# Reordering VectorE's and ScalarE's steps in the 16x64 attention layers: turned copies first, combining multiply last, copy of the last pair ahead of the exps

## What is computed

```python
h = (x - mu) * rsqrt(var + eps) * ln_scale + ln_bias
q, k, v = up-projections of h @ w_down_q.T and h @ w_down_kv.T, (b, 16, s, 64)
q, k = rope(q), rope(k)
scores = einsum('bhqd,bhkd->bhqk', q, k) / sqrt(64)
attn = softmax(scores, axis=-1)
out = einsum('bhqk,bhkd->bhqd', attn, v)
out = out.reshape(b, s, 1024) @ w_out.T + residual
```

## Time and profile before

| | |
|---|---|
| time, median of 3 runs | 2920.61 us (2910.09 to 2923.78) |
| the profiled execution | 2914.34 us, its span 2912.6 us |
| PE busy | 2224.6 us (76%) |
| DVE busy | 1690.1 us (58%) |
| ACT busy | 1174.3 us (40%) |
| POOL busy | 522.7 us (18%) |

### The profile page before, as it was taken

How to read it: one execution, slowest core, us unless ns; L and a number is a source line. 1 busy time by engine, 2 the same in 40 slices (tenths; PEclk the granted TensorE clock), 3 DMA queues, 4 the chain that set the end, 5 groups by cost and what they waited for, 6 DMA issues and landing times. The chain is left out here.

```text
span 2912.6 us, 40706 instructions
## 1 busy us (share of the span) xinstructions
PE 2224.6 (76%) x13779; PEld 1382.4 (47%) x13779; DVE 1690.1 (58%) x3810; ACT 1174.3 (40%) x2898; POOL 522.7 (18%) x703
## 2 busy tenths in 40 slices
PE   4668888789996897534799994936888886898982
PEld 2424343367774454423566663625555654344441
DVE  5568999633434562877456556562665554754524
ACT  3114444445552564211344441410555553354550
POOL 1122220000002410121111101011333322212100
PEclk9759999899997898866899997965999998698995
DMA  0043323110002310000000001011000001332200
GB/s 27 12 116 86 115 77 92 50 40 1 1 1 62 76 46 28 8 0 0 31 1 1 1 1 28 1 27 34 1 1 1 1 1 38 85 75 63 53 11 17
DMA packets 109272, 95.63 MB, mean 33 GB/s; under 512 B 61414, under 2 KB 96526, under 8 KB 105742
## 3 DMA queue, kind: packets, MB, share of 16 engines
q1 hardware_dynamic: 75790, 91.99, 12.2%
q10 hardware_dynamic: 33280, 1.05, 0.5%
HBM read 77.21 MB, written 14.81 MB: 32 GB/s over the span
## 5 line engine op out<-in xcount | busy, mean ns | idle before, releaser
L920 DVE TENSOR_REDUCE L_xattn_mx<-L_xattn_psS 128x1 f32<-128x512 f32 x512 | 326.9, 684 | 152.9 <-PE L_xattn_psS L1045 148.7
L1160 ACT ACTIVATE L_xattn_PT<-L_xattn_psT 128x512 f32<-128x512 f32 x512 | 284.7, 598 | 170.8 <-PE L_xattn_psT L1057 163.6
L1071 PE MATMUL L_xattn_psO<-L_xattn_PT,L_xattn_V 128*32 128x256 f32 x2048 | 264.1, 404 | 40.8 <-DVE L_xattn_PT L931 40.8
L588 ACT ACTIVATE L_attn_pr<-L_attn_psS,L_attn_negm 128x256 f32<-128x256 f32 (+1 forms) x512 | 222.4, 447 | 175.4 <-PE L_attn_psS L511 92.0
L1045 PE MATMUL L_xattn_psS<-L_xattn_KR,L_xattn_QR 72*128 72x512 bf16 x512 | 224.0, 441 | 56.3 <-DVE L_xattn_mx L920 30.0
L1057 PE MATMUL L_xattn_psT<-L_xattn_QR,L_xattn_KR 75*128 75x256 bf16 x1024 | 198.7, 283 | 3.0 <-ACT L_xattn_PT L1160 2.0
L1875 DVE TENSOR_TENSOR L_ffn_wt<-L_ffn_act,L_ffn_cw 128x512 f32<-128x512 f32 x128 | 88.5, 692 | 183.8 <-ACT L_ffn_act L1992 172.4
L1071 PEld LDWEIGHTS L_xattn_psO<-L_xattn_PT,L_xattn_V 128*32 128x32 f32 x2048 | 118.4, 115 | 154.6 <-issue 61.2
L931 DVE SCALAR_TENSOR_TENSOR L_xattn_PT<-L_xattn_PT,L_xattn_floor_w 128x512 f32<-128x512 f32 x256 | 178.4, 741 | 16.1 <-DMA L_xattn_floor_w<-L_xattn_staged_floor 11.6
L392 DVE TENSOR_REDUCE L_attn_mx<-L_attn_psS 128x2 f32<-128x512 f32 x256 | 164.4, 684 | 40.0 <-PE L_attn_psS L501 40.0
L415 DVE TENSOR_TENSOR L_attn_aoT<-L_attn_raw,L_attn_psOR 128x256 f32<-128x256 f32 x128 | 54.0, 422 | 222.7 <-ACT L_attn_raw L601 222.7
(11 more groups left out here) (537 smaller groups left out, 4342.8 us busy)
## 6 DMA issues: line engine op xcount, KB each, us to landing
L_xattn_KR<-L_xattn_k_parts SPq DMA_DIRECT2D x96, 192.0 KB
L_xattn_floor_w<-L_xattn_staged_floor SPq DMA_DIRECT2D x8, 2048.0 KB, 8.2
L_xattn_QR<-L_xattn_q_parts SPq DMA_DIRECT2D x32, 288.0 KB
L_xattn_k_parts<-L_xattn_ks SPq DMA_DIRECT2D x48, 128.0 KB, 2.6
L_xattn_ctxT<-in_ctx SPq DMA_DIRECT2D x24, 192.0 KB, 2.4
L_attn_QR<-L_attn_q_parts SPq DMA_DIRECT2D x16, 288.0 KB
L_attn_KR<-L_attn_k_parts SPq DMA_DIRECT2D x48, 96.0 KB
L_xattn_q_parts<-L_xattn_qs SPq DMA_DIRECT2D x48, 64.0 KB, 2.5
```

What stands on the lines that cost most here:

```text
L588: ins = nc.scalar.activation(pr[n % 3][:, r, t, 0:width], psS[(2 * n + r) % 3][:, t, 0:width], ACT.Exp, bias=negm[:, n % 4, t, r:r + 1], s ...
L920: nc.vector.reduce_max(mx[:, b % 2, u, hd:hd + 1], psS[n % 2][:], AX.X).then_inc(s_used, 1)
L1071: ins = nc.tensor.matmul(psO[r:r + HW, g % 2], V[b % NV][:, kt, n % H], PT[(n * NU + kt // 2) % NPT][:, kt % 2], start=(kt == 0), stop=(kt ...
L1160: nc.scalar.activation(PT[i % NPT][:], psT[i % NPS][:], ACT.Exp).then_inc(exp_ready, 1)
```

## The change

VectorE's step becomes `copy_turned(n-2)` (causal), `maxima(n)`, the reads, `invert(n-1)`, `combine(n-2)`, and then the moments where the step has them: the multiply comes last in the step, and it is the pair n-2 instead of n-3. ScalarE's step becomes (`copy_turned(n-2)` in the layer that is not causal), the reads, `copy_out(n-2)`, `exps(n)`: the last two change places. No instruction is added or removed, and the orders of TensorE, GpSimd and SyncE stay. The two layers share the function, so both change.

```diff
@@ VectorE @@
             for n in range(FIRST, LAST):
-                if 0 <= n - 3 < NN:
-                    combine(n - 3)
                 if causal and 0 <= n - 2 < NN:
                     copy_turned(n - 2)
                 if 0 <= n < NN:
...
                 if 0 <= n - 1 < NN:
                     invert(n - 1)
+                if 0 <= n - 2 < NN:
+                    combine(n - 2)
                 b, at = n // NP + 2, n % NP
@@ ScalarE @@
                     for job in group:
                         read(job)
+                if 0 <= n - 2 < NN:
+                    copy_out(n - 2)
                 if 0 <= n < NN:
                     exps(n)
-                if 0 <= n - 2 < NN:
-                    copy_out(n - 2)
```

## The result

The changed kernel takes 2933.88 us (median of 7 runs, 2933.12 to 2941.62) against 2916.97 us before (7 runs, 2910.09 to 2923.78), a ratio of 1.0064 with a 95% interval of 1.0048 to 1.0080. Measured once more beside other runs of the kernel before it was 2938.06 against 2915.19, ratio 1.0085 (1.0071 to 1.0099). So it is slower, by 17 to 23 us; 26 were forecast. In absolute time the forecast was 2947 us: 2933.88 lies in its range of 8 in 10 (2929 to 2967) and at the foot of the forecast's own (2934 to 2962). 3.6 us of the distance are the base, 2920.61 us in the three runs that the forecast started from and 2916.97 in seven. The first profile of the changed kernel has a span of 2938.7 us, 26.1 more than before, the second one 2932.0.

What follows compares the result with a forecast made beforehand. The prediction took a circle through ScalarE's copy and VectorE to bound causal plain steps, and TensorE the other layer. Causal -11.8 and other +38 made +26 on 2920.61, so 2947 us, 8-in-10 range 2929 to 2967.

Steps and rivals of the forecast that it cites:

- Both readings: Causal plain steps: a closed circle (exps, copy, multiply, turned copies, maxima, mask, exps), 5.23 us; other layer: TensorE never idles, 4.19.
- The new path, 0.48 + 0.25 + 1.06 or 1.17: `spread_inverse` to copy, copy to exps, exps to next `scores`: 1.79 us in the causal layer, 1.90 in the other.
- The causal layer, -11.8: Sum for the causal layer over plain, T, V or O steps and last pairs: -11.8 us, ends -6 and -15.
- Plain steps: Causal layer, steps without a V job: 4.62 us against 5.23, -0.61 each in 16 steps, -9.8.
- T steps: Causal layer, 7 steps with a T job: two transposes add 0.44 us, so -0.2 each, -1.2.
- (c): Causal layer, 37 steps with V or O, TensorE's own: 1.79 us for 1.73, +0.06 each, +2.2.
- The end of the layer: Causal layer's last pairs, with no projection, circle-bound throughout: between 0 and -4 us, taken as -3.
- The other layer, 61 x 0.65 = 39.7: Non-causal layer, steps n = 2 to 62: `spread_inverse` to next `scores` from 1.25 to 1.90 us, +0.65 each, +39.7.
- the clock: Non-causal layer: some nine steps lose 1.6 us at the lower clock; part of the new wait lies under it, -2.
- the second rival: Non-causal layer: steps fall differently and slow stretches go, 9 x 1.6 = 14.4 us less, 2933; chance 0.06.
- The first rival: Non-causal layer: new 0.65 gap puts six more V and seven T steps at low clock, +21 us, 2968; chance 0.12.
- The rival on the other side: Non-causal layer: earlier multiply brings VectorE's P bank reads forward, returning 48 us of TensorE's waits, 2899; chance 0.07.

Runs made afterwards that it cites:

- the wait alone: Kernel before, with the non-causal layer's exps of pair n also waiting for `spread_inverse(n-2)`, copy still behind them: 2941.31 us, ratio 1.0094.
- the doubled copy: Changed kernel with ScalarE's copy made twice in the non-causal layer, first into a spare tile, both ahead of exps: 2957.00 us against 2938.06.
- The runs with `weigh` moved: Non-causal layer's `weigh` and `spread_inverse` ahead of V, T, C jobs: 2866.03 us on kernel before, 2850.22 with the copy between the heads, 2879.03 on changed kernel.
- the copy between the heads: Kernel before, with ScalarE copying pair n-2 between first and second head's exps of pair n, in both layers: 2898.44 us, ratio 0.9947.

## Why the prediction was right, and where it was off

What bounds a step. Both readings held: one engine's part alone showed the circle over ScalarE's copy in the causal layer, and in the other the wait alone and the doubled copy showed that what is put ahead of the exps is paid in every step.

The new path, 0.48 + 0.25 + 1.06 or 1.17. Measured 0.48, 0.27 and 1.06 (1573.71, 1574.19, 1574.46, 1575.52), and 0.47, 0.27 and 1.17 in the other layer. Right to 0.02.

The causal layer, -11.8. It gave -14.3, with the terms off both ways. Plain steps are 4.73 and not 4.62: `spread_inverse` comes 2.92 after `scores` and not 2.83, since from the P job to `weigh` it is 1.06 where no V job stands between (1571.85 to 1572.91, the P job of the step shown above), and I had put 0.97, the distance from P to V. That is 16 x 0.11 = 1.8 less. T steps are 4.95 for 5.06 forecast, since the two transposes add 0.22 to a plain step and not 0.44: 7 x 0.11 = 0.8 more. V steps are 5.59 for 5.57 forecast, 0.7 less over the 37 steps of (c). The seven steps with V and O went from 7.55 to 7.38, not to 7.61: V had waited for VectorE's read of the O bank (the weight load of V idles 0.39 us for it at n = 27, and not at all after the change), which was late because of the circle, and I had counted that as TensorE's own time; 7 x 0.23 = 1.6 more. The end of the layer gave 5.6 (1.0 in the last step, 4.6 after it) where I took 3, an estimate with little under it.

The other layer, 61 x 0.65 = 39.7. Taking out the excess of the slow V steps over the others of their kind, it is 378.2 before (392.6 less nine of 1.6) and 417.4 in the second profile (420.9 less 0.95, 0.97 and 1.58): +39.2.

The step that failed in size is the clock. I took nine slow V steps to stay nine and put -2 for them. They were seven in one profile and three in the other, with 9.0 and 3.5 us lost in them in place of 14.4. So the term was -5 and -11, and with the causal layer's 2.5 that covers what the forecast of 26 was too high by; it goes part of the way to the second rival, which I gave 0.06. Probably this is more than the chance of two executions: the four profiles in which the plain step of this layer has its old 4.18 and `weigh` its old place show eight or nine slow V steps, the four with the change three, four, four and seven. Why there are fewer stays open, and the kernels with the wait alone and with the doubled copy, at ten and eight, do not have fewer. The first rival, more slow steps for the new gap in every step, did not occur.

The rival on the other side had it that VectorE's reads, and with them 48.3 us of TensorE's waits, would come earlier. They didn't: TensorE waits 30.6 us in 15 for V as before. The change does not move the multiply in VectorE's queue, as this rival has it. In time it does come earlier, released by the earlier copy (it starts at 2237.30 and the next `scores` at 2238.26, n = 31), and the reads come no sooner for it. The runs with `weigh` moved show that most of the 48 us are there to be had: the wait ahead of V falls to 10.2 us in 15, those ahead of T and C go, and the steps get 36 us shorter. It is TensorE's order that holds them, not VectorE's.

What I did not see is that the VectorE part of the diff is no move at all but for the moments. The forecast was not hurt by it, since its sum costs ScalarE's order alone and gives the multiply's move no term.

## What to carry to other kernels

An instruction with a late wait should not stand ahead of the one that releases the bounding engine; put it behind the first such release (here between two heads), where it costs neither engine. The same edit can cut a circle in one variant of a shared function and hang the pace on TensorE's last task in another, so make such orders conditional and read one step of each variant. And before costing a move, count its place in the queue in both versions: a change of step together with a change of index can be no move.

## What the runs showed of the hardware

A gap of 2.07 us in TensorE's work before V brings the clock down to 1.2 GHz in some steps and not in others of the same kind: nine of fifteen in the kernel before, eight with the causal layer changed alone, eight with VectorE's part alone (in six of its V steps the gap is 2.7, and two of these six fell), nine with the copy between the heads, three, four, four and seven in the four profiles with the change in this layer, ten with the wait alone (its gap is 2.24), eight with the doubled copy. Which ones fall I could not foresee from the step. With the gap at 0.69 none fell, in all three kernels that have it. The Trainium skill, page "TensorE: Matmul & The Clock Gate", section "HAM oscillation", names idle gaps as the cause, and the 1.00 of those runs agrees; but the gap of its example is a wait of 3 to 5 us for a transfer. Here a gap of 2.07 was enough in some steps, and the measurement decides. An idle of 0.60 in every step did not bring the clock down by itself: the plain steps of the changed kernel all take 4.85 or 4.86.

ScalarE starts the next instruction 0.25 to 0.27 us after a copy of 128x256 whose own duration is 0.37: in a chain on this engine the distance between starts is the price, not the duration.
